# Query projection of a decoder layer in tiles of 128 tokens across batches, with a later start of the first weight preparation

## The reference

```python
x = x + attn(layernorm(x))            # 16 heads of 32, rotary, causal
x = x + xattn(layernorm(x), ctx)      # the part that the change touches
x = x + ffn(layernorm(x))             # ternary weights, silu gate, rms norm

# xattn, with xq_v = fp8(ln(x) / scale_v) for each of the four projections v
q  = ln(xq_q @ wq);  k  = ln(xq_k @ wk);  v  = xq_v @ wv      # self part "S"
qx = ln(xq_x @ wqx); kx = ln(ctx @ wkx);  vx = ctx @ wvx      # context part "X"
out = fp8(concat(softmax(q k') v, softmax(qx kx') vx) / smooth) @ wproj
```

## Time and profile before

| | us |
|---|---|
| median of three runs | 1265.29 (1263.04 to 1266.21) |
| the profiled execution | 1269.15, with a span of 1267.4 |
| busy: TensorE matmul | 1200.4 (95%) |
| busy: VectorE | 932.4 (74%) |
| busy: ScalarE | 806.3 (64%) |
| busy: GpSimd | 607.4 (48%) |
| mean granted TensorE clock | 0.973 |

### The profile page before, as it was taken

One profiled execution on the slowest core, in us unless ns is written; L12 is line 12 of the kernel. 1 busy time (PEld: TensorE's weight loads), 2 busy tenths in 40 slices (PEclk: granted clock), 3 DMA queues, 4 the chain that ended last, 5 costly groups with the idle time before them and its releaser, 6 DMA issues.

```text
span 1267.4 us, 19410 instructions
## 1 busy us (share of the span) xinstructions
PE 1200.4 (95%) x6432; PEld 820.7 (65%) x6432; DVE 932.4 (74%) x2794; ACT 806.3 (64%) x2301; POOL 607.4 (48%) x722
## 2 busy tenths in 40 slices
PE   3899989889999999999999999999999998999998
PEld 1577767556666666676666777776667765555545
DVE  4667897999888887799999966657777877463341
ACT  4576557767877776676667765566787676652230
POOL 0656794654453455555555732124454534363370
PEclk8899898889999999999999999999999999899999
DMA  8420000011210221113233221041111100000000
GB/s 262 133 67 1 2 1 1 1 34 54 65 51 18 62 80 58 56 62 104 87 108 96 61 79 38 17 141 58 44 32 58 46 31 1 1 1 11 20 1 29
DMA packets 25460, 65.60 MB, mean 52 GB/s; under 512 B 2720, under 2 KB 8992, under 8 KB 25360
## 3 DMA queue, kind: packets, MB, share of 16 engines
q1 hardware_dynamic: 25088, 64.00, 16.1%
q10 hardware_dynamic: 272, 0.36, 0.1%
HBM read 59.37 MB, written 4.98 MB: 51 GB/s over the span
## 4 chain that ended last, share of the span: by engine, by line
PE 63%; DVE 19%; ACT 11%; POOL 3%; issue 2%; DMA 1%; ACTq 0%; POOLq 0%; SPq 0%
PE ps L855 14%; PE ps L1052 8%; PE ps L1119 8%; PE ps L845 6%; PE ps L1014 5%; PE ps L947 5%; PE ps L1168 4%; PE ps L504 3%; ACT big L785 3%; PE ps L979 3%; DVE big L967 3%; PE ps L796 2%; DVE big L412 2%; PE ps L569 2%; PE ps L616 1%
## 5 line engine op out<-in xcount | busy, mean ns | idle before, releaser
L855 PE MATMUL ps<-big 128*125 128x512 bf16 x1152 | 264.5, 379 | 0.5 <-ACT big L942 0.5
L785 ACT ACTIVATE big<-ps,big 112x128 f32<-112x128 f32 (+1 forms) x512 | 192.4, 456 | 72.8 <-POOL big L430 70.2
L855 PEld LDWEIGHTS ps<-big 128*125 128x125 bf16 x1152 | 155.2, 136 | 80.3 <-ACT big L942 0.8
L429 POOL TENSOR_TENSOR big<-big 112x4 f32<-112x4 f32 (+1 forms) x128 | 38.4, 300 | 319.9 <-ACT big L424 319.8
L845 PE MATMUL ps<-big 128*112 128x512 bf16 x768 | 188.4, 389 | 2.9 <-ACT big L942 2.0
L659 POOL TENSOR_TENSOR big<-big 128x448 f32<-128x448 bf16 x96 | 101.7, 1060 | 116.6 <-DVE big L964 69.7
L845 PEld LDWEIGHTS ps<-big 128*112 128x112 bf16 x768 | 100.1, 133 | 67.1 <-issue 7.0
L967 DVE TENSOR_SCALAR big<-big 112x112 f32<-112x112 f32 (+1 forms) x256 | 131.5, 534 | 6.8
L412 DVE BATCH_NORM_STATS2 big<-ps 112x6 f32<-112x128 f32 (+1 forms) x512 | 113.3, 283 | 20.1 <-PE ps L855 18.8
L950 ACT ACTIVATE big<-ps,big 112x375 f32<-112x375 f32 x128 | 74.6, 583 | 82.6 <-DVE big L949 81.5
L1014 PE MATMUL ps<-big 125*128 125x224 f32 (+1 forms) x512 | 121.8, 361 | 4.3 <-DVE big L996 3.5
(11 more groups left out here) (115 smaller groups left out, 2316.1 us busy)
## 6 DMA issues: line engine op xcount, KB each, us to landing
big<-in_ctx_t SPq DMA_DIRECT2D x32, 375.0 KB, 3.7
big<-in_w_s SPq DMA_DIRECT2D x16, 512.0 KB, 3.8
big<-in_w_p SPq DMA_DIRECT2D x16, 512.0 KB, 3.8
big<-in_w_x SPq DMA_DIRECT2D x16, 512.0 KB, 3.9
big<-in_w_g SPq DMA_DIRECT2D x16, 512.0 KB, 4.0
big<-in_w_d SPq DMA_DIRECT2D x8, 512.0 KB, 4.5
big<-in_w_a SPq DMA_DIRECT2D x8, 384.0 KB, 5.2
scr<-big SPq DMA_DIRECT2D x24, 128.0 KB, 1.7
```

Of the source, the lines that this page charges most:

```text
L785: t = act(lambda e, j=j: e.activation(z[0:rows, 128 * j:128 * j + 128], bk[0:rows, 128 * j:128 * j + 128], ACT.Identity, bias=rr[0:rows, 4 ...
L855: t = pe(lambda e, k=k, s=s, u=u, n=n: e.matmul(bk[0:CK, :], cT[:, s, k, CK * c:CK * c + CK], w[:, u, k, col:col + 512], start=n == 0, sto ...
```

## The change

q (and the self part's k) no longer come batch by batch. The 896 tokens are projected in 7 tiles of 128, so a tile i holds the end of batch i and the beginning of batch i+1. A batch's turns stay as many; where there was an eighth item, the turn's item is now "n" and does nothing.

- In S the items of batch b's four turns are now: k of tile b-1, q1 of tile b-1, q0 of tile b, v of batch b. In X the eight turns have q1 of tile b-1, q0 of tile b, k0 to k2, v0 to v2, and X0 begins with one more "n". Seven tiles in place of eight batches take away 10 items: those of S0's turns 0, 1 and 30, S1's 32, 33 and 62, X0's 65 and 122, X1's 129 and 186. Turn 64 holds X0's extra "n"; the last item of X1 moves into turn 192, which had none.
- All of X's items come one turn later against the attention than before (v2 of a batch was two turns ahead of its first scores' turn, and is now one).
- The eviction L802 of a tile becomes two instructions, one for each batch, each with a token in that batch's `ready`. q has a ring for each half of the heads (`qh`) in place of `qr`, of the same size.
- `load_ctx` is called in the turn of q1 (tile b-1), in front of the new order's k0 by two turns as before, and one turn later in X than it was.
- `s0prep` moves on by single steps from step 6 on, and by two from step 10 on.

```diff
-        qr = Ring([f32(rings.take(896), 896).rearrange("p (h t) -> p h t", h=8) for _ in range(2)])
+        aQ = rings.take(1792)
+        qh = [Ring([f32(aQ + 896 * i + 448 * c, 448).rearrange("p (h t) -> p h t", h=4) for i in range(2)])
+              for c in range(2)]
...
-            dst, free_dst = it["dst"]()
             b3 = bk[:, 0:4 * rows].rearrange("p (g t) -> p g t", g=4)
-            tf = act(lambda e: e.activation(dst, b3, ACT.Identity, bias=bb, scale=w), t, free_dst, t_qsb)
+            for bt, dst, free_dst, lo, hi in it["dst"]():
+                tf = act(lambda e, dst=dst, lo=lo, hi=hi: e.activation(dst, b3[:, :, lo:hi], ACT.Identity, bias=bb,
+                                                                       scale=w), t, free_dst, t_qsb)
+                bt["ready"] += [tf]
             bank.release(bi, tf)
-            it["batch"]["ready"] += [tf]
...
+                bts = hf["batches"] = [dict(hf=hf, b=b, ready=[], k=hf["kind"]) for b in range(NB)]
                 for b in range(NB):
-                    seq = ["q0", "q1", "k0", "v0"] if hf["kind"] == "S" else \
-                        ["q0", "q1", "k0", "k1", "k2", "v0", "v1", "v2"]
+                    seq = [("k", 0, b - 1), ("q", 1, b - 1), ("q", 0, b), ("v", 0, b)] if S else \
+                        [("q", 1, b - 1), ("q", 0, b)] + [("k", c, b) for c in range(3)] \
+                        + [("v", c, b) for c in range(3)]
+                    if hf["name"] == "X0" and b == 0:
+                        seq = [("n", 0, 0)] + seq
+                    for n, (what, c, i) in enumerate(seq):
+                        tile = what == "q" or (S and what == "k")
+                        if tile and not 0 <= i < NB - 1:
+                            what = "n"
+                        it = dict(hf=hf, b=i, what=what, c=c, tile=tile, ctx=bts[b] if not S and n == 0 else None)
...
         def p_mm(it):
+            if it["ctx"]:
+                load_ctx(it["ctx"])
+            if it["what"] == "n":
+                return
...
-                xq = xqx[:, :, T * b:T * b + T] if v == 3 else xqv[:, v, :, T * b:T * b + T]
+                rows = 128 if it["tile"] else T
+                sl = slice(rows * b, rows * b + rows)
+                xq = xqx[:, :, sl] if v == 3 else xqv[:, v, :, sl]
+                toks = [xq_tok[(v, b)], xq_tok[(v, b + 1)]] if it["tile"] else xq_tok[(v, b)]
...
+            def tile_dst():
+                b, key = it["b"], ("q", c) if it["what"] == "q" else "kk"
+                own = T - 16 * b
+                res = []
+                for to, at, lo, hi in ((bt, 16 * b, 0, own), (it["nxt"], 0, own, 128)):
+                    if key not in to:
+                        to[key] = (qh[c] if it["what"] == "q" else kS).take()
+                    _, a, af = to[key]
+                    res.append((to, a[:, :, at:at + hi - lo], af, lo, hi))
+                return res
...
-            if n >= 3:
+            if n >= 6:
                 next(s0prep, None)
-            if n >= 4:
+            if n >= 10:
                 next(s0prep, None)
...
-        n_items = len(pitems)
+        n_items = len(aitems) - 1
```

More of the change, by code:

```diff
@@ L808, in proj_items @@
             for hf in halves:
+                S = hf["kind"] == "S"
+                bts = hf["batches"] = [dict(hf=hf, b=b, ready=[], k=hf["kind"]) for b in range(NB)]
                 for b in range(NB):
-                    bt = dict(hf=hf, b=b, ready=[], k=hf["kind"])
-                    hf.setdefault("batches", []).append(bt)
-                    bt["n"] = 4 if hf["kind"] == "S" else 8
-                    seq = ["q0", "q1", "k0", "v0"] if hf["kind"] == "S" else \
-                        ["q0", "q1", "k0", "k1", "k2", "v0", "v1", "v2"]
-                    for s in seq:
-                        items.append(dict(batch=bt, hf=hf, b=b, what=s[0], c=int(s[1])))
+                    seq = [("k", 0, b - 1), ("q", 1, b - 1), ("q", 0, b), ("v", 0, b)] if S else \
[8 more added lines that the diff above has]
+                        it = dict(hf=hf, b=i, what=what, c=c, tile=tile, ctx=bts[b] if not S and n == 0 else None)
+                        if what != "n":
+                            it.update(batch=bts[i], nxt=bts[i + 1] if tile else None)
+                        items.append(it)
             return items
@@ L834, in p_mm @@
             w = hf["w"]
-            if it["what"] == "q" and c == 0 and not S:
-                load_ctx(bt)
             bi, (bk, _), free = bank.take()
@@ L845, in p_mm @@
                         t = pe(lambda e, k=k, s=s, n=n: e.matmul(
-                            bk[0:T, :], xq[:, k, :], w[:, s, k, col:col + 512], start=n == 0, stop=n == 7),
-                            xq_tok[(v, b)], free, ready[hf["name"]][k], signal=n == 7)
+                            bk[0:rows, :], xq[:, k, :], w[:, s, k, col:col + 512], start=n == 0, stop=n == 7),
+                            toks, free, ready[hf["name"]][k], signal=n == 7)
                         n += 1
-                rows = T
             else:
@@ L879, in p_z @@
         def p_z(it):
+            if it["what"] not in "qk":
+                return
             hf, bt, c = it["hf"], it["batch"], it["c"]
             S = hf["kind"] == "S"
-            if it["what"] == "v":
-                return
             lnb_z(it)
@@ L927, in t_s0 @@
             S = bt["k"] == "S"
-            qi, q, _ = bt["q"]
+            half = g // 2
+            qi, q, _ = bt["q", half]
             ki, kk, _ = bt["kk"]
@@ L952, in t_s0 @@
             bank.release(bi, te)
+            if g % 2 and (S or it["hh"]):
+                qh[half].release(qi, t)
             if it["last"]:
-                qr.release(qi, t)
                 (kS if S else kX).release(ki, t)
```

39 lines of the change are left out of this document (15 added, 24 removed).

## The result

The changed kernel takes 1296.30 us (median of 4 runs, 1295.47 to 1298.37), the kernel before, run beside it, 1264.47 (4 runs, 1263.04 to 1266.21). The ratio is 1.025, with an interval of 1.024 to 1.027: 32 us slower, where 12.7 us less were forecast, and outside of the range. The profiled execution took 1296.46, with a span of 1294.4.

What follows compares the result with a forecast made beforehand. TensorE was taken as the bound (63% of the chain), fully so in X1. Terms -17.3 - 1 + 3 - 4 + 8.6 + 3 - 5 = -12.7 gave 1252.6 us against 1265.29, range 1242 to 1266 (its own 1245 to 1260, chance 0.55).

Steps and rivals of the forecast that it cites:

- `load_ctx` at nothing: In X, the context's load one turn later costs nothing: k0 is still two turns off, covered by TensorE work.
- Matmuls, -17.3: Projections on TensorE: ten items of 8 matmuls less, 0.216 us each, tiles of 128 no dearer: -17.3 us.
- What VectorE keeps, +3: Border of S0 and S1: VectorE is late next, so 3.0 of TensorE's 6.9 us are not gained; 0 to 6.
- A stall that goes, -4: S0's first turns: the projection's 3.62 us wait for GpSimd's queue goes with turns 0 and 1 empty; 0 to -9.
- A wait that comes, +8.6: X: head 0's scores wait for the v2 copy, 0.54 us later, 16 times: +8.6 us.
- Two evictions for one, +3: ScalarE: a tile's two evictions take 0.90 us, 0.29 more; ten steady S batches 0.3 later each, nothing in X; 0 to 8.
- The first preparation, -5: Start of the kernel: casts come after the first q and GpSimd's rotary, up to 6.1 us earlier; -9 to +2.
- Rival 2: X: scores wait for a whole ScalarE queue, 5.6 us in some five batches: +25, 1277.7 us; chance 0.10.
- Rival 1: X: the v copy is hidden, so the 8.6 us wait does not come: 1244.0 us; chance 0.12.
- rival 3: Start: early gains don't hold, VectorE fills the start, turn 3 stalls as turn 1 did: +9, 1261.6 us; chance 0.18.
- Rival 4: Empty turns let TensorE's clock fall; four turns at half speed cost 1.9 us each: 1260.2 us; chance 0.05.
- The prediction's own sign of error: It is wrong if X's batches lengthen by over 1 us each, or the main loop's first projection doesn't come earlier.

Runs made afterwards that it cites:

- e11: The changed kernel without the context's subtraction on VectorE, except in X0's first batch: 1277.14 us.
- e3: The changed kernel with X's items ordered q0, k0 to k2, q1, v0 to v2: 1305.41 us (1.030).
- e2: The changed kernel, scores waiting only for k and their own half of q, the product with v for v: 1291.25 us (1.019).
- e13: The changed kernel with X0's two streams of background work (X1 weight preparation, spilled FFN weights) one turn later: 1288.52 us (1.017).
- e4: The changed kernel with the edits of e1 and e2 together: 1252.98 us (0.989 of the kernel before).
- e14: Tiles of 128 in S alone, X's q in tiles of 112 at the turns of before, new pace, waiting lists apart as in e4: 1254.91 us (0.990).
- e1: The changed kernel with all items of X projected one turn earlier: 1253.67 us (0.990 of the kernel before).
- e12: e1 without the context's subtraction on VectorE, except in X0's first batch: 1252.90 us.
- e7: The kernel before with the first preparation's new pace alone: 1260.20 us (0.997).
- e8: e1 with the first preparation's pace of before: 1258.78 us (0.996 of the kernel before).
- e9: e1 with five unused VectorE subtractions more per X batch, in the turn of head 0 behind the quantisation: 1300.98 us.

## Why the prediction was wrong, point by point

The step that failed is **"`load_ctx` at nothing"**, and behind it one omission: the change moves every item of X by one turn against the attention and the background work, and the prediction followed this shift for one instruction, the v2 copy. For `load_ctx` it asked when k0 needs the result, which was right, and not what the subtraction that comes with it holds up on VectorE: without it X is 23.2 us shorter (589.1 in e11 for 612.3), half of the 47.2. In the table the loss falls into four places: the context's subtraction behind the quantisation, 1.7 us in each batch (e11); the q1 tile's eviction in the turn ahead of head 4, 0.8 in X0 and 0.6 in X1 (the turn of head 3 in e11 against that in e3, which is 5.33 in X0); the v2 copy, 0.53 (e2); in X0 alone k2's statistics behind background work, 1.36 (e13). In X1 these are 2.8 of the 3.1. In X0 they are 4.4 of the 4.7; why the turn of head 7 is 0.4 longer in X0 than in X1 (9.52 and 9.09) no run explains.

- **Matmuls, -17.3.** The price of a matmul held (389 ns). At the border of S0 and S1 three items' worth came, less what VectorE kept (next point). In X, where TensorE was busy without a break and the whole should have been gained, the four items bring some 2 us even in e4. There the gain shows at the borders: X0's last two batches are 3.3 us shorter than before (the 3.9 in e14's expectation is e1's), X1's last but one 2.1, and what follows X1 is 2.9 longer (205.8 for 202.9). Of these, 1.0 is a longer wait of TensorE at the start of a group of matmuls behind X, L1189 (3.54 us idle for 2.53), and 1.7 a difference in clock: behind a later wait of 2.29 us, the same in both, the clock is 0.51 from 1215.0 to 1218.4 in e4 and stays at 1.00 before. e1 and e12 show the same two steps, e14 neither.
- **What VectorE keeps, +3.** Right: the three batches at the border of S0 and S1 took 49.8 us before and 45.8 now, 4.0 less, where 6.9 - 3.0 = 3.9 stood.
- **A stall that goes, -4.** Most of it moved. The idle time of 4.17 at the earlier trace rows is down to 1.13 us, but S0's first scores, behind the k tile's eviction, wait in its place; so do those of the next two batches:

```profile
187.61 0.60 PE L685 MATMUL ps<-big 112*128 112x112 f32 x4 [1.13 <-ACT big L787]
...
188.96 3.25 PE L862 MATMUL ps<-big 128*128 128x512 bf16 x8
...
205.02 0.81 PE L954 MATMUL ps<-big 128*112 128x112 f32 x4 [2.91 <-ACT big L804]
...
224.61 1.09 PE L954 MATMUL ps<-big 128*112 128x112 f32 x4 [5.09 <-ACT big L804]
...
244.42 1.09 PE L954 MATMUL ps<-big 128*112 128x112 f32 x4 [4.80 <-ACT big L804]
```

  1.13 and 2.91 together are 4.04, close to the one wait of before, and the 8 matmuls behind the first still run at half speed. e7, with the same pace and nothing else, gives the account: against it the first scores come 3.4 us earlier (205.0 for 208.4) and the three batches behind take 1.0 less, 4.4 in all, where the stall and the matmuls of turns 0 and 1 (16 at 0.216) were to bring 7.5. The prediction covered k's tile by "that turn's 16 matmuls"; in S0's first three batches no output projection stands there yet. What these waits cost by themselves is open: VectorE is busy for 24.28 of 25.00 us just ahead of them, and the k tile was not tried apart.
- **A wait that comes, +8.6.** Right in place, count and size: 16 times, 0.53 us each by e2, for 0.54.
- **Two evictions for one, +3.** The pair takes 1.00 us, for 0.90. Steady S batches got 0.1 to 0.2 longer (17.0 for 16.9, 16.4 for 16.2), half of the term, but not by the wait that was named: the idle time in front of S's scores that L785 ended, 0.47, is down to 0.25 behind its successor L787. "In X nothing follows" was wrong: the q1 tile's pair stands right ahead of head 4.
- **The first preparation, -5.** Right: 4.75 and 5.1 (e7, e8). The first q and GpSimd's rotary start at 23.98 and 24.73 us for 31.32 and 32.09:

```profile
23.98 1.27 DVE L518 TENSOR_TENSOR big<-ps,big 112x512 f32<-112x512 f32 x2
...
24.73 1.26 POOL L532 TENSOR_TENSOR big<-big 112x512 f32<-112x512 f32 x1 [24.31 <-DVE big L518]
```

- **The rivals.** Rival 2 had the sign, but not the mechanism: the scores never stood behind a whole queue of ScalarE, which waited for v2 itself (5.19 us in the timeline above). Rival 1 falls with e2, rival 3 in part (the stall stayed, the pace held). Rival 4 did not happen in X's batches: the clock was 1.00 there through idle times of 0.8 us. At the borders, where the empty turns lie, it did in some executions. e13 has the code of the changed kernel up to X0; at the end of S1 TensorE waits in both for 0.58, 0.7 and 1.20 us, and behind that a window of e13 and one of the changed kernel show two clocks:

```profile
446.30:453.10 6.80, 5.92 (x18) 3.27 (x19) 6.62 (x19) 2.60 (x10) 5.62 (x5) 0.50 0.68 230
...
446.30:453.10 6.80, 6.74 (x36) 4.26 (x36) 6.59 (x24) 2.69 (x12) 5.48 (x6) 1.00 0.59 216
```

  The batch took 18.2 us in e13 and 15.3 in the changed kernel. At the border of S0 and S1 the clock fell in e2, e4 and e14 (a batch of 17.8 for 16.1) and not in the others; in the kernel before and in e7 it did not fall between S0's fourth batch and X1's last. So the rival was right that the empty turns can cost clock, but in the profiled execution of the changed kernel nothing of this was paid at either border. The prediction's own sign of error, batches of X longer by more than 1 us, was the right one to look at first.

That the sum came near the result of e1 and e4 (1252.6 forecast, 1253.67 and 1252.98 measured) is no merit of it: there the wait of 8.6 is not paid, and the matmuls of X and the stall did not bring what was put down for them.

## What to carry to other kernels

Where a change shifts one stream of work by a step against another, list all that the stream issues on every engine and write down in which step of the other each now lands: the instruction that costs may be one that the change never meant to touch. Here a moved piece was free only in the step where another engine was the late one, only as long as it fitted there (1.8 us did, 2.1 more did not), and it needed a step of distance to its first reader. A loop that repeats shows this when its steps are timed one by one: each edit then changes one or two columns, where the total mixes them with waits and clock elsewhere.

## What the runs showed of the hardware

- A short wait of TensorE cost more than its recorded idle time: in X1's steady batches 0.37 us recorded at the scores behind the v2 copy, 0.53 in the turn (e2); matmuls around the waits read longer instead (the scores' mean is 498 ns, in e4's X1 479). The Trainium skill, page "TensorE: Matmul & The Clock Gate", section "Step-by-step: what each phase is for", has the drain of one matmul overlap the fill of the next, so that a stream hides it and a lone matmul can't. That the 0.16 us are this no run here shows.
- Here VectorE's subtractions and GpSimd's elementwise instructions held each other up. GpSimd's L662, 1.03 us by itself, took 3.26 beside the context's subtraction (timeline above), and 2.92 and 1.36 in turn in X0's steady batches, before 1.36 and 1.04; the subtraction itself kept its 0.93. In e9 it is the other way: subtractions of 0.42 us took 1.14 beside L661 and L662, which themselves took 1.30 and 1.10. The Trainium skill, page "SBUF — State Buffer", section "SBUF: two separate sides", has VectorE's operations with two SBUF inputs and GpSimd's exclude each other, the one that starts first going first. The trace agrees in e9, where the subtractions, which started 0.44 and 0.24 us behind the other, are held up most. In the changed kernel the one held up is recorded as starting 0.05 us ahead; spans on GpSimd are rough, so this is no clear case against it.
- The same waits of TensorE let the clock fall in one execution and left it alone in another: 0.58, 0.7 and 1.20 us at the end of S1 (0.50 in e13, 1.00 in the changed kernel), 2.29 us behind X (0.51 in e4, 1.00 in the kernel before).
